# Streaming a matrix in two 64 KB-row loads per group through two buffer slots, in place of three loads through three

## The reference

```python
# x: 8192 x 64, adj: 8192 x 8192, w: 8192, W_agg: 64 x 64, all fp32
agg = adj @ (x @ W_agg)
y   = w[:, None] * relu(agg) + (1 - w)[:, None] * x
out = layernorm(x + y)          # mean and variance over 64 columns, eps 1e-5
```

## Time and profile before

| | us |
|---|---|
| time, median of three runs | 638.72 |
| time of the profiled execution | 638.89 |
| span of the profiled execution, first to last instruction | 637.0 |
| TensorE busy (matmul) | 519.5 (82%) |
| VectorE busy | 55.8 (9%) |
| ScalarE busy | 15.9 (2%) |
| bytes read from HBM | 270.60 MB |
| DMA rate over the span | 428 GB/s |
| granted TensorE clock, mean | 0.912 of full speed |

### The profile page before, as it was taken

The page is one execution under the profiler, slowest core; times in us unless marked ns, Lnnn a source line. Parts: engine busy times, 40 slices in busy tenths (PEclk is TensorE's granted clock), DMA queues, the critical chain, the costliest instruction groups (busy, mean ns, idle before and its releaser), DMA issues.

```text
span 637.0 us, 5371 instructions
## 1 busy us (share of the span) xinstructions
PE 519.5 (82%) x2304; PEld 177.2 (28%) x2304; DVE 55.8 (9%) x136; ACT 15.9 (2%) x35; POOL 0.3 (0%) x5
## 2 busy tenths in 40 slices
PE   0678798878987888797878977878887987978996
PEld 0123232222222322222222322322222222222345
DVE  2000101010010100101001010100101001010102
ACT  0000000000000000000000000000000000000000
POOL 0000000000000000000000000000000000000000
PEclk9997898888979889897988979898888989888999
DMA  9999999999999999999999999999999999999998
GB/s 362 453 418 453 419 427 433 425 447 428 444 414 447 419 429 443 441 432 419 451 410 436 436 450 423 427 431 425 446 424 453 424 429 419 436 444 420 428 413 349
DMA packets 9667, 272.75 MB, mean 428 GB/s; under 512 B 1472, under 2 KB 1728, under 8 KB 3008
## 3 DMA queue, kind: packets, MB, share of 16 engines
q1 hardware_dynamic: 9360, 272.63, 99.6%
q10 hardware_dynamic: 304, 0.07, 0.1%
HBM read 270.60 MB, written 2.10 MB: 428 GB/s over the span
## 4 chain that ended last, share of the span: by engine, by line
DMA 69%; PE 29%; issue 0%; SPq 0%; ACT 0%; DVE 0%; DVEq 0%
DMA ring<-adj_main_dram 69%; PE bank L156 29%; PE bank L164 0%; SPq L114 0%; ACT aggT L203 0%; ACT aggT L208 0%; SPq L110 0%; SPq L109 0%; DVE res L267 0%; ACT std_last L199 0%; DVE y_last L261 0%; ACT aggT L211 0%; DVE stats L263 0%; DVE y_last L262 0%; DVE mv L264 0%
## 5 line engine op out<-in xcount | busy, mean ns | idle before, releaser
L156 PE MATMUL bank<-ring,x_sb 128*64 128x512 f32 (+2 forms) x2176 | 501.7, 621 | 102.2 <-DMA ring<-adj_main_dram 102.1
L156 PEld LDWEIGHTS bank<-ring,x_sb 128*64 128x64 f32 x2176 | 161.6, 148 | 430.2 <-issue 299.7
L245 DVE SCALAR_TENSOR_TENSOR y<-bank,w_sb 128x256 f32<-128x256 f32 (+1 forms) x16 | 6.7, 420 | 552.7 <-PE bank L164 552.7
L164 PE MATMUL bank<-wagg,aggT 128*128 128x64 f32 x128 | 17.9, 281 | 11.2 <-ACT aggT L203 10.3
L164 PEld LDWEIGHTS bank<-wagg,aggT 128*128 128x128 f32 x128 | 15.6, 191 | 25.4 <-ACT aggT L203 23.5
L203 ACT COPY aggT<-bank 128x512 f32<-128x512 f32 x15 | 8.8, 585 | 527.0 <-PE bank L156 527.0
L234 DVE TENSOR_TENSOR y<-y,res 128x256 f32<-128x256 f32 (+1 forms) x16 | 6.7, 420 | 2.2
L242 DVE TENSOR_TENSOR res<-y,rstd 128x256 f32 (+1 forms) x16 | 6.7, 421 | 0.6
L238 DVE TENSOR_TENSOR sq<-y 128x256 f32<-128x256 f32 (+1 forms) x16 | 6.7, 421 | 0.6
L236 DVE SCALAR_TENSOR_TENSOR y<-rowsum,y 128x256 f32<-128x256 f32 (+1 forms) x16 | 6.7, 420 | 0.5
L239 DVE TENSOR_REDUCE varsum<-sq 128x4 f32<-128x256 f32 (+1 forms) x16 | 6.7, 416 | 0.5
(11 more groups left out here) (9 smaller groups left out, 1.3 us busy)
## 6 DMA issues: line engine op xcount, KB each, us to landing
ring<-adj_main_dram SPq DMA_DIRECT2D x30, 5632.0 KB, 27.2
ring<-adj_main_dram SPq DMA_DIRECT2D x15, 5120.0 KB, 29.8
ring<-adj_mid_dram SPq DMA_DIRECT2D x2, 2304.0 KB, 22.8
ring<-adj_mid_dram SPq DMA_DIRECT2D x1, 3072.0 KB, 21.5
ring<-adj_mid_dram SPq DMA_DIRECT2D x2, 1536.0 KB, 23.9
x_sb<-x_dram SPq DMA_DIRECT2D x1, 2048.0 KB, 8.0
out_dram<-res SPq DMA_DIRECT2D x1, 2016.0 KB, 8.1
ring<-adj_last_dram SPq DMA_DIRECT2D x2, 768.0 KB, 23.0
```

The costliest lines, as they stand in the source:

```text
L156: last = nc.tensor.matmul(into[j % 2 * D:(j % 2 + 1) * D, 0:cols], x_sb[:, j], ring[:, at + s * cols:at + (s + 1) * cols], start=j < 2, st ...
L164: last = nc.tensor.matmul(rows[:, i * D:(i + 1) * D], aggT[:, i * P:(i + 1) * P], wagg2[:], start=True, stop=True)
L245: step(nc.vector.scalar_tensor_tensor(out=y[:, 0:n], in0=rows.rearrange("p (n d) -> p n d", d=D), scalar=0.0, in1=over_row(w_sb[:, bass.ds ...
```

## The change

One line of numbers is changed:

```diff
-MAIN_LOADS = (22, 22, 20)
+MAIN_LOADS = (32, 32)
 MID_LOADS = (16, 12, 12, 8, 8, 4, 2, 2)
 LAST_LOADS = (10, 12, 12, 10, 7, 5, 4, 2, 2)
```

## The result

The changed kernel takes 658.6 us (median of four runs, 656.56 to 661.15) against 639.17 for the kernel before on the same chip: a ratio of 1.031, 95% interval 1.029 to 1.033. The forecast was 645.0 us with a range up to 649. The sign was right, the size wrong by a factor of three. The profiled execution of the changed kernel is its fastest, 656.56 us, with a span of 654.7 us; 17.7 us more than before.

The account below looks back on a forecast made before the run. The DMA rate was taken to bound the stream, with TensorE's work after the last main landing added. The terms 5.2 + 1.4 - 0.3 + 0 = +6.3 us gave 645.0 us, range 642.6 to 649.

Parts of the forecast that it names:

- The bound and its two terms: Whole kernel: time is the landing of the last main load, set by DMA rate, plus TensorE's work from there.
- Term 1: Matmuls left after the last main landing: 32 steps instead of 20 at full clock, uncovered, +5.2 us.
- Term 2: Clock on the last main load: its first steps may run at half clock after idle time, +1.4 us (0 to 2.9).
- Term 3: The loads' own overhead: fifteen loads fewer at 0.02 us each, -0.3 us (0 to -1.5).
- The depth of the queue: Streaming loads, two slots: one load covers a refill, slack 1.0 to 2.4 us, cost 0, with 2 us kept for the range.
- Rival A: Streaming loads: the queue runs dry at every load, 0.5 us each, 659 us; chance 0.12 together with small packets.
- Its second branch: Main loads: 64 KB rows are cut into small packets and move slower, 666 us; within the shared chance of 0.12.
- Rivals B and C: B: dropping fifteen loads gives back a serial piece, 620 us, chance 0.03. C: longer tail hidden, around 639 us, 0.03.
- The clock: TensorE's slow start after idle: +1.4 us on the last main load, 2.9 us on the worst load in the queue's count.

Follow-up runs that it names:

- the last experiment: Changed kernel plus matmuls that nothing reads in TensorE's idle time, written in turn to both halves of their PSUM bank: 642.4 us, ratio 1.0044.
- the five runs of the table: Changed kernel (658.6 us); with 2, 5 or 8 matmul steps of each load left out (654.1, 642.5, 640.9); with added matmuls alternating between bank halves (642.4).
- the first run with added matmuls: Changed kernel plus matmuls that nothing reads in TensorE's idle time, all written to one half of their PSUM bank: 671.3 us.

## Why the prediction was wrong

**The bound and its two terms: right.** The time is the landing of the last main load plus TensorE's work from there. Behind the landing, the steps have the durations of the earlier trace rows without holes.

**Term 1, +5.2 us: right.** At full clock the last load takes 13.95 us in the last experiment against 8.80, +5.15.

**Term 2, +1.4 us: right.** The last load of the changed kernel took 15.57 us, 1.6 over 13.95, and its head ran at half clock (columns as in the earlier trace rows):

```profile
603.22:606.62 3.40, 3.40 (x10) 1.01 (x12) 0.00 (x0) 0.00 (x0) 0.00 (x0) 0.51 1.00 419
```

Together the end cost 6.6 us, as forecast. (One count was short: the merged row of before at 75.61 us, 84 matmul rows in 21.18 us, holds a seventh load that paid over 2.4 us for the clock. It changes nothing in the sum.)

**Term 3, -0.3 us: too small.** With fifteen loads fewer and no losses after the start-up the last main load starts at 590.83 instead of 591.95, -1.1 us; with fifteen more, +1.05. A load costs 0.07 us of its own, not 0.02, within the bounds of 0 to 0.1 that the rounding left.

**The depth of the queue, 0 with 2 us kept for the range: wrong, and this is the whole miss.** It cost 12.4 us in the profiled execution (603.22 against 590.83). The medians are 16.2 us apart (658.6 against 642.4), of which the 1.6 of term 2 are the clock on the last load; 14.6 are left. The step that failed reads "So 1.0 to 2.4 us of slack are left on a mean load and the queue doesn't run dry". The count behind it was nearly right in each number: TensorE's mean load took 15.6 us (467.3 us over 30 loads) against 15.3 forecast, the fixed time of a DMA is 2.4 to 2.8 us against 1.7 to 3.1, and the last engine was on average 3.8 us from its end when a refill was issued. What it left out is that sixteen engines move a load, each with an end of its own. It took the landing, which is the end of the last engine, for the moment when the DMA engines run out of work, and on the other side started TensorE from that same last end. The first engine was through 0.7 to 2.6 us before the last. On average it had only 2.2 us left at the issue, and from 3 us on nothing was lost in any of the five runs of the table. Against that mark the slack was not +1.0 but -0.8 us. The spread itself had no row; a full queue hides it. In the kernel before, the packet records have one engine some 2 us behind the first while the loads stay 13.33 us apart. That lateness of the refill is what costs the time is shown by the runs; that the spread is what the count lacked rests on the packet records alone, and thirteen refills, issued 1.6 to 1.9 us ahead without a loss, don't follow from it. What exactly decides the size of a loss stays open.

The losses are also larger where it counts than "each lost 0.5 us in six loads": in the changed kernel 12 of 27 refills lost over 0.1 us, up to 2.1, and 12.6 in all.

**Rival A** named the mechanism, a refill that comes too late, and its price, 659 us, is close to the measured 658.6. That is in part luck: it had 0.5 us lost at every load for a longer fixed time, where 15 of 27 refills lost next to nothing and the others up to 2.1 us. It got 0.12, because it was put to a fixed time of over 4.1 us, which no row gave. The fixed time measured lies inside the bounds; what was missing was the spread of the engines' ends. Its second branch, rows cut into small packets, is out: the packet records have one packet for a row.

**Rivals B and C** did not come. B's serial piece is 0.07 us a load, not 0.44, so the page "SBUF — State Buffer" of the Trainium skill (section "The DMA setup-cost knee") is borne out here only for a DMA into an empty queue, where 2.4 to 2.8 us stand beside its 2.

**The clock** was priced in the tail and as the worst load of the queue's count, but not as what decides that count. It does: with TensorE at full clock every refill from 121 us on was issued 3.0 us or more before the first engine was through, and none of them lost over 0.04 us.

## What to carry to other kernels

When a change takes a buffer slot away from a stream that the DMA rate bounds, don't compare the consumer's time with the time of the other load. Compare it with that time less the landing and issue (0.6 us here), less 3 us for the next transfer to be flowing, less the spread between the sixteen engines (0.7 to 2.6 us here): 19.35 us of cover bore about 14 us of matmuls here, not 16. The 3 us are the safe side of these runs and not a constant; one run got by with 1.6. And price the consumer at the clock that it will have with the new idle time in front of each load. The load left when the stream ends is paid in full, but cutting it shorter pays only until the data behind it is what ends last.

## What the runs showed of the hardware

An engine that falls behind stays behind as long as the queue stays full. In the kernel before, one engine fell back once, at the time of a transfer of 16 KB on the instruction queue that took 1.1 us at 43.9 us. From then on the spread between the first and the last engine's end was about 2 us for the rest of the stream, where it had been 0.5; fifteen of the sixteen stayed within 0.7 us. In the kernel with loads of 36 and 28 steps, whose queue ran empty once a group, the spread stayed at 0.4 to 0.7 us.

How a late refill costs time can be read in the packet records, in two forms. In the first run with added matmuls, the refill issued at 308.82 us met engines that were all through by 0.2 us after it. They began its packets 1.0 to 1.5 us after the issue, all within 0.5 us, and these first packets took 2.9 to 3.3 us in place of 2.42. In the changed kernel, the refill issued at 143.69 us met ten engines that were through by 145.6 us and six that were not. The first packet began 1.8 us after the issue, but some idle engines got their first one only 2.8 to 3.2 us after it, and twelve of the sixteen first packets took 2.7 to 4.1 us. In other refills of that kernel idle engines began up to 4.0 us after the issue. That is of the size of the 3 us above. With rows of 32 KB the slowest first packet took 3.13 us in place of 1.21, so what is added, 1.7 and 1.9 us at worst, was not larger for the longer row. The records don't name the engines. Whether one that is served last was idle for longer or only slowed by the others, and why half of the refills issued latest of all lost nothing at the landing, stays open; no run here separates these.

A 512-column fp32 step takes TensorE 0.43 us when the steps alternate between the two halves of its columns, and 0.83 us (7.46 for nine) when they all go to one half, at the same granted clock of 1.00.
